# DLRM tower on one core: what GpSimd waits for before it gathers the next tile's rows

## What is computed

```python
e = jnp.stack([tbl_0[ids[:, 0]], ..., tbl_26[ids[:, 26]]], axis=1)     # 2048 x 27 x 128
interactions = jnp.einsum('bfd,bgd->bfg', e, e)
z = jnp.concatenate([e.reshape(B, -1), interactions[:, _TRIU_I, _TRIU_J]], axis=1)
h = jnp.concatenate([z, dense_ctx], axis=1)
h = jnp.maximum(h @ W_top1 + b_top1, 0.0)      # 3823 -> 512
h = jnp.maximum(h @ W_top2 + b_top2, 0.0)      # 512 -> 256
y = h @ W_top3                                 # 256 -> 1
```

## Time and profile before

| | us |
|---|---|
| median of three runs | 729.75 (729.03 to 732.96) |
| the profiled execution, its own time | 727.98 |
| its span, from the first to the last instruction | 726.0 |
| TensorE matmul busy | 538.2 (74%) |
| GpSimd busy | 413.0 (57%) |
| VectorE busy | 374.4 (52%) |
| ScalarE busy | 237.2 (33%) |

### The profile page before, as it was taken

How to read it: one execution, slowest core, us unless ns; L and a number is a source line. 1 busy time by engine, 2 the same in 40 slices (tenths; PEclk the granted TensorE clock), 3 DMA queues, 4 the chain that set the end, 5 groups by cost and what they waited for, 6 DMA issues and landing times.

```text
span 726.0 us, 8455 instructions
## 1 busy us (share of the span) xinstructions
PE 538.2 (74%) x2688; PEld 492.7 (68%) x2688; DVE 374.4 (52%) x1218; ACT 237.2 (33%) x721; POOL 413.0 (57%) x438
## 2 busy tenths in 40 slices
PE   0721687978877787878878797878878797878974
PEld 0621576868777686768777686767777686767863
DVE  3412562836456372736456382736547382736573
ACT  3312432424142332425142332425142332425240
POOL 5775466566656566566656566566656566562000
PEclk9955898999999999999999999999999999999995
DMA  6732311111111111111111111111111111110000
GB/s 200 224 108 68 92 47 48 37 44 47 48 38 48 40 45 47 39 47 44 48 39 49 41 45 45 40 48 44 48 36 48 44 44 45 41 47 23 1 0 0
DMA packets 19470, 37.84 MB, mean 52 GB/s; under 512 B 7668, under 2 KB 8692, under 8 KB 19428
## 3 DMA queue, kind: packets, MB, share of 16 engines
q0 software_dynamic: 13824, 28.34, 15.0%
q1 hardware_dynamic: 5316, 8.72, 3.7%
q10 hardware_dynamic: 288, 0.26, 0.1%
HBM read 37.28 MB, written 0.01 MB: 51 GB/s over the span
## 4 chain that ended last, share of the span: by engine, by line
PE 49%; another core or an unknown queue 18%; DVE 14%; issue 10%; ACT 6%; DMA 2%; POOL 1%; ACTq 0%; DVEq 0%
PE ps_acc L215 13%; PE ps_acc L216 10%; PE ps_acc L217 9%; PE ps_gram L247 7%; PE ps_t L209 6%; DVE g_buf L434 4%; DVE emb_x L418 3%; DVE g_buf L428 3%; ACT emb_x L345 2%; ACT g_buf L377 2%; DVE h_lo L470 1%; PE ps_late L260 1%; ACT w_hi L336 1%; PE ps_late L277 1%
## 5 line engine op out<-in xcount | busy, mean ns | idle before, releaser
L196 POOL DMA_INDIRECT emb<-in_tbl,idx x432 | 412.3, 954 | 246.1 <-issue 117.8
L215 PE MATMUL ps_acc<-w_hi,emb_x 128*128 128x512 f32 x432 | 205.9, 477 | 39.9 <-issue 36.4
L428 DVE COPY g_buf<-ps_gram 32x112 f32<-32x112 f32 x512 | 141.3, 276 | 97.5 <-PE ps_gram L247 35.1
L216 PE MATMUL ps_acc<-w_lo,emb_x 128*128 128x512 f32 x432 | 175.8, 407 | 0.0
L217 PE MATMUL ps_acc<-w_hi,emb_x 128*128 128x512 f32 x432 | 174.6, 404 | 0.0
L377 ACT ACTIVATE g_buf<-ps_gram 32x112 f32<-32x112 f32 x512 | 130.4, 255 | 120.7 <-PE ps_gram L247 54.6
L418 DVE TENSOR_TENSOR emb_x<-ps_t,emb_x 128x512 fp32r<-128x512 f32 (+1 forms) x112 | 74.4, 664 | 184.6 <-ACT emb_x L345 139.2
L215 PEld LDWEIGHTS ps_acc<-w_hi,emb_x 128*128 128x128 f32 x432 | 130.8, 303 | 47.6 <-issue 42.8
L216 PEld LDWEIGHTS ps_acc<-w_lo,emb_x 128*128 128x128 f32 x432 | 135.2, 313 | 0.6
L345 ACT ACTIVATE emb_x<-ps_t 128x512 fp32r<-128x512 f32 (+1 forms) x112 | 63.7, 582 | 211.9 <-PE ps_t L209 142.0
L217 PEld LDWEIGHTS ps_acc<-w_hi,emb_x 128*128 128x128 f32 x432 | 131.9, 305 | 1.4
(11 more groups left out here) (34 smaller groups left out, 286.3 us busy)
## 6 DMA issues: line engine op xcount, KB each, us to landing
g_buf<-in_W_top SPq DMA_DIRECT2D x31, 256.0 KB
emb<-in_tbl,idx POOLq DMA_INDIRECT x432
g_buf<-in_W_top SPq DMA_DIRECT2D x1, 222.0 KB
idx<-in_ids SPq DMA_DIRECT2D x1, 216.0 KB, 5.3
b_rows<-in_b_top ACTq DMA_DIRECT2D x1, 128.0 KB, 4.8
w_rows<-in_W_top ACTq DMA_DIRECT2D x1, 128.0 KB, 5.9
ctx_rows<-in_dense_ctx SPq DMA_DIRECT2D x4, 32.0 KB
g_buf<-in_b_top SPq DMA_DIRECT2D x1, 2.0 KB
```

The source lines that it names most:

```text
L196: pool.indirect_dma_start(out=emb[:, f * D:(f + 1) * D], out_offset=None, in_=tables[f], in_offset=bass.IndirectOffsetOnAxis(ap=idx[:, t, ...
L215: pe.matmul(acc, x_hi, w_hi[0:rows, c, lo:hi], start=start, stop=False)
L216: pe.matmul(acc, x_hi, w_lo[0:rows, c, lo:hi], start=False, stop=False)
L428: last = dve.tensor_copy(target, source)
```

## The change

GpSimd's waits are replaced. No gather, no transfer and no instruction of another engine is added, taken out or put in another order.

- g0 of tile t waits until tile t-1 is split as a whole (`s_emb_lo` at 7t); g1 follows with no wait.
- g2, g3 and g4 wait for 4, 9 and 14 gram units of tile t-1.
- g5 and g6 wait for the products of g0 and of g1 of tile t itself.

```diff
+            UNITS_BEFORE = {2: 4, 3: 9, 4: 14}
             for t in range(TILES):
                 for g in range(NG):
                     if t > 0:
-                        pool.wait_ge(s_pe_t, NG * (t - 1) + g + 1)
+                        if g == 0:
+                            pool.wait_ge(s_emb_lo, NG * t)
+                        if g in UNITS_BEFORE:
+                            pool.wait_ge(s_gram, UNITS * (t - 1) + UNITS_BEFORE[g])
+                        if g in (5, 6):
+                            pool.wait_ge(s_emb_mm, NG * t + g - 4)
                     for f in GROUPS[g]:
                         pool.indirect_dma_start(
```

## The result

The changed kernel takes 830.64 us (median of 4 runs, 821.15 to 840.55); the kernel before took 731.36 us beside it (4 runs, 729.03 to 734.87). The ratio is 1.128, with a 95% interval of 1.121 to 1.136. The prediction said 813 us in a range of 710 to 855, slower with a chance of 0.70.

A forecast was written before the change was run, and what follows sets the result against it. TensorE's updates, held beside GpSimd's gathers, were taken as the bound. Tile 1's first gram unit 109, 14 periods of 47.5 (to 665), and 35.4 gave 809.4 of span; with 2.0 and 1.8 added, 813 us, range 710 to 855.

The forecast's parts named there:

- narrower forecast: Whole kernel: updates let out one at a time, periods of 46.5 to 50 us, 799 to 851 us; chance 0.55.
- What bounds the kernel: Middle tiles: beside GpSimd's gathers, news of TensorE's end reaches other engines late, some 6.5 us of a 40.99 us period.
- Held updates: During long gather runs: TensorE's finished work reported late to other engines, one update at a time, 3.5 us apart in the forecast.
- Start: Tiles 0 and 1: GpSimd stops behind 27 gathers, bringing tile 1's first gram unit to about 109 from 120.96.
- Steady period: Middle tiles: 16 gathers in one 20 us run over the gram phase hold updates; period 47.5 us taken, 49.9 alternative.
- free stretch: Opening part of a gather run, before updates are held: 6 us gives period 49.9, 10 us gives 47.5.
- first case: Middle tiles, 6 us unheld: next tile's first product at +27, columns' turn held 2.4 us, period 49.9 us.
- Sum: Whole kernel: 109 to tile 1's first gram unit, 665 for 14 periods, 35.4 to the end: 809.4 us span.
- Light holding: Rival, whole kernel: openings release everything pending or come often; period 40.5 us, about 712 us; chance 0.2.
- no change: Rival, whole kernel: gathers aren't what delays updates, or effects cancel; 728 to 732 us; chance 0.06.
- Nothing held: Rival, middle tiles: no updates held, GpSimd's own loop sets a 37.3 us period; 667 us in all; chance 0.03.
- the last rival: Gram phase: the 20 us run releases no update from +10 until a pause; period 51 to 52, 865 us; chance 0.1.

The follow-up runs named there:

- second trace of the changed kernel: The changed kernel itself, run again unchanged beside the kernel before on a holding chip: 826.61 us (4 runs), ratio 1.116.
- g0 and g1 back: Changed kernel, but g0 and g1 wait as in the kernel before, for turns of the tile before: 813.51 us, ratio 1.109, on a holding chip.
- the run with the memset: Changed kernel with a one-byte GpSimd memset behind each gather, on a free chip: 645.75 us beside 616.69, ratio 1.048.
- g0's wait alone: Kernel before, with g0 also waiting until the tile before is split as a whole: 1037.34 us, ratio 1.412, on a holding chip.

## Why the prediction was right

The time lies in the range, 710 to 855 us, but that range took in the rival at 712 as well, so this alone says little. The narrower forecast, periods of 46.5 to 50 us and 799 to 851 us (0.55), is what held.

**What bounds the kernel: right, for holding chips alone.** Held updates, in an order of one at a time, are in every trace of a holding chip, and gathers are their cause. I hadn't thought that the kernel before itself could take 617 us. Two readings of rows were wrong. The last tile isn't "the same work": it has 160 products where a middle one has 169, so the gathers' price was 5.8 us a tile and not 6.5. And tile 0's long run has 43 gathers, not 44 (27, and 16 of tile 1 up to the wait of g4), which is 1.25 us.

The Trainium skill (SBUF — State Buffer, section "Who interferes with whom") says that PE and ACT never wait on anyone. Free chips agree, with 35.2 us a tile with gathers and without. But the section speaks of ports of SBUF, and what is late on holding chips is the news of a finished instruction, so I had weighed it against something that it doesn't deny.

**Start: right in direction, too small.** I had tile 1's first gram unit at 109, 105 at the least. It came at 102.90, and at 105.09 in the second trace of the changed kernel. ScalarE in tile 0, and TensorE's first gram unit of tile 1:

```profile
37.42 0.60 ACT L353 ACTIVATE emb_x<-ps_t 128x512 fp32r<-128x512 f32 x1 [14.83 <-remote]
...
44.60 0.60 ACT L353 ACTIVATE emb_x<-ps_t 128x512 fp32r<-128x512 f32 x1 [4.50 <-PE ps_t L217]
...
102.90 0.49 PE L255 MATMUL ps_gram<-emb_x 128*128 128x224 f32 x2 [0.19 <-DVE emb_x L426]
```

g4 is split at 44.60 where I said 49. I had taken the release of g3 at 46 from the long run of gathers; it came at 37.42, inside the run of 27. The start gained 18 us of 121, and it is all the change gains.

**Steady period: the mechanism right, the case chosen wrong.** I worked out 49.9 us with a free stretch of 6 us, and took 47.5 with one of 10. The mean is (802.30 - 102.90) / 14 = 49.96. The first late update comes at +7.1, as in the earlier trace rows, behind a pause of 12.44 us. So the step that failed is "since GpSimd would now have a pause of some 10 us ahead of each run": a longer pause doesn't lengthen the free stretch. The steps of the first case stand: copies at +7 and +10, no 14 units at +20, the first product at +27 (479.82 - 452.1 = 27.7), the columns' turn at +38. **That the 47.5 us came near was luck:** eight of the 14 periods are 48.0 us, but by other steps, a first product at +27.7 and not +22, and columns that aren't held. These rows are TensorE's turn of the columns and ScalarE's reading in the tile of 53 us, and in the one of 48:

```profile
490.10 0.49 PE L268 MATMUL ps_late<-ident,cols 128*128 128x128 f32 x3
...
543.22 0.49 PE L268 MATMUL ps_late<-ident,cols 128*128 128x128 f32 x3
```

```profile
543.75 0.38 ACT L360 ACTIVATE cols_hi<-ps_late 128x256 fp32r<-128x256 f32 x1 [2.70 <-issue]
```

490.10 - 452.1 = 38.0, and 543.22 - 505.1 = 38.1. In the tile of 48 the columns aren't held (read 0.53 us later), and 9.9 us bring the next tile: 38.1 + 9.9 = 48.0. In the tile of 53 they are read at 493.08, 2.98 us after the turn begins, so 2.45 are held, as the 2.4 of my first case. That gives 50.4, and 53.0 was measured.

Which tiles are held here goes with GpSimd's rows. The run of seven begins at 536.84 in the tile of 48:

```profile
536.84 1.46 POOL L204 DMA_INDIRECT emb<-in_tbl,idx  x1 [2.48 <-PE ps_acc L225]
```

Its first gather takes 1.46 us, where that of the tile of 53, at 483.17, takes 0.94. In both traces of the changed kernel all 18 tiles from tile 1 to 14 that begin this run with a gather of 1.36 to 1.70 us have columns that aren't held, and all ten that begin it with one of 0.94 or 0.95 have held ones. Other traces agree: the run of the earlier trace rows has a second gather of 1.17 us, and that at 472.37 with g0 and g1 back a first one of 1.37, and both let relu through at once 10 us in. Tile 1 was thus a row of another kind, and not a longer free stretch after a longer pause. What makes such a gather long, and why nothing is held behind it, stays open.

**Of the missing 2.6 us the clock, which I had left out, explains 2.3.** TensorE's granted clock in stretches of these tiles, behind the columns:

```profile
492.10:496.10 4.00, 1.67 (x4) 1.41 (x5) 1.22 (x3) 1.04 (x3) 0.00 (x0) 0.66 0.06 16
496.10:500.10 4.00, 4.00 (x10) 3.05 (x10) 0.00 (x0) 0.60 (x1) 0.00 (x0) 0.50 0.00 0
...
545.10:549.10 4.00, 4.00 (x17) 3.63 (x18) 0.45 (x1) 0.60 (x1) 0.91 (x1) 1.00 0.12 35
```

Where TensorE had stood still for 3.4 us behind the held columns, the clock is at 0.50 (1.2 of 2.4 GHz) to about 500, and the 512-wide products go 0.43 us apart in place of 0.235: 12 such steps (495.00 to 500.12) x 0.19 = 2.3 us. The tile of 48 has no stop there and stays at 1.00. In the gram phase the clock is at 0.50 in both, from 468 to 476 in the tile of 53, and that is inside its 27.7 us. Eight of the 14 periods are of 48 us, three of 52.1 and three of 53.0: 6 x 4.6 = 27 us of span come from tiles in which the columns are held too.

**Sum.** 102.90 + 14 x 49.96 + 36.2 (802.30 to 838.5) = 838.5. Against my 109 + 665 + 35.4: the start 6 us less, the periods 34 us more, the end 1 us more. The first case's 49.9 with the start as measured gives 837; it had the size of the periods almost exactly, but through errors that cancelled: held columns in every tile (they are held in six of 14), 9.5 us behind them where it is 9.9, and no loss of clock. This sum is of the traced execution, 10 us above the median. How many tiles are held differs from one execution to the next: in the second trace of the changed kernel (831.13 us) it is four of 14, and the mean period 49.1 us.

**The rivals.** Light holding (712) and no change fall on a holding chip. "Nothing held" had its floor right (37.2 against 37.3 us a tile), but it belongs to another chip, and there, measured with the memset, it is a loss, 1.048, since the kernel before is then at 35.2 us a tile (by its variants). I had given it as a gain, to 667 us, since I compared a changed kernel without holding with the kernel before with it. So the change is slower on both kinds of chip, for two different reasons, the second as far as the run with the memset stands for it. That a long run over the gram phase lets out less and less, the last rival, is what g0's wait alone shows at 1037 us; in the changed kernel g4's wait ends the run before that.

## What to carry to other kernels

A wait moved to a later event can be harmless for its own data and still cost, by gathering instructions into one long run and by what that run then lies beside: ask of each moved wait how long the run behind it becomes and which hand-overs fall in it. A loop that is closed through one buffer (gather, turn, split, and gather again) has a period that can be added up from rows; if it is above the other engines' period, the wait that closes it costs, even on a quiet chip. Where the chain names "another core or an unknown queue" on one core, run the kernel before again elsewhere before you explain it, and put what is to be compared into one kernel if the place can't be chosen. If a variant with an added load looks free, see whether the loaded engine keeps up or only falls behind within the stretch.

## What the runs showed of the hardware that I had not expected

- The same kernel took 731 to 736 us (medians) on some chips and 617 to 620 us on others, with single runs of a group within 1% of each other. What makes the difference, the chip or the moment, isn't shown by any run.
- On the first kind, TensorE's semaphore updates came late beside GpSimd's indirect DMAs. Only ScalarE, VectorE and GpSimd have rows that are ended by "remote"; in no trace has TensorE one. The profile models the end of a matmul, so these rows can't tell a late update from a late last write of the results; TensorE's own next products went on meanwhile (in the tile from 452.07, to 461.4). Inside a run of 27 the spacing grew from 3.5 to 8.4 us and was then 5.6. They were all let out some time after its end, and that time grew with the run: 1.4 us after 7 gathers, 1.7 after 8 (462.24 to 463.91), 2.2 after 12, 2.9 after 16, 4.7 after 27 (533.69 to 538.35), 5.7 after 43 (from the earlier trace rows and the rows above).
- Neither memsets, 20.74 us of them a tile, nor plain DMAs at 53 GB/s had any such effect on the same chip.
- From tile 1 on, a run of gathers with one of 1.17 to 1.70 us among its first three, instead of 0.95, let updates through for 10 us; runs without one held them from about 6 to 7 us on. The cause isn't known.
- Held updates cost twice: the stop itself (3.4 us of TensorE), and then products 0.43 us apart instead of 0.235, at a granted clock of 0.50.
